# A gated cross-attention and ternary feed-forward kernel: normalised x split into bf16 halves before it is transposed, and transposed by DMA instead of on TensorE

## The reference

```python
def _L0_xattn_ref(hidden_states, encoder_hidden_states, Wq, Wk, Wv, Wo, gq, gk):
    q = (hidden_states @ Wq).reshape(B, Sq, H, D)          # 32 sequences of 100 rows, 512 wide; 16 heads of 128
    k = (encoder_hidden_states @ Wk).reshape(B, Skv, H, D) # 361 context rows, 256 wide
    v = (encoder_hidden_states @ Wv).reshape(B, Skv, H, D)
    q = rmsnorm(q, gq)
    k = rmsnorm(k, gk)
    scores = jnp.einsum('bqhd,bkhd->bhqk', q, k) * scale
    attn = jax.nn.softmax(scores, axis=-1)
    out = jnp.einsum('bhqk,bkhd->bqhd', attn, v)
    return out.reshape(B, Sq, H * D) @ Wo
x = x + jnp.tanh(g_xattn[0]) * _L0_xattn_ref(_layernorm(x, axis=-1), ctx_1024, ...)
x = x + jnp.tanh(g_ffn[0]) * _L0_ffn_ref(_layernorm(x, axis=-1), ...)
```

## Time and profile before

| | |
|---|---|
| time, median of 3 runs | 2481.73 us (2481.36 to 2483.34) |
| the profiled execution's own time | 2482.65 us |
| its span, first to last instruction | 2480.5 us |
| PE busy | 2256.4 us, 91% |
| DVE busy | 1903.3 us, 77% |
| ACT busy | 1577.8 us, 64% |
| POOL busy | 1200.9 us, 48% |
| float32 transposes of x on TensorE | 128, 18.0 us busy |
| mean granted TensorE clock | 0.970 of full |

### The profile page before, as it was taken

One profiled execution on the slowest core, in us unless ns is written; L12 is line 12 of the kernel. 1 busy time (PEld: TensorE's weight loads), 2 busy tenths in 40 slices (PEclk: granted clock), 3 DMA queues, 4 the chain that ended last, 5 costly groups with the idle time before them and its releaser, 6 DMA issues. The chain is left out here.

```text
span 2480.5 us, 52473 instructions
## 1 busy us (share of the span) xinstructions
PE 2256.4 (91%) x16482; PEld 1597.2 (64%) x16634; DVE 1903.3 (77%) x4175; ACT 1577.8 (64%) x3226; POOL 1200.9 (48%) x1538
## 2 busy tenths in 40 slices
PE   2599999999999999999999999999999995589998
PEld 1377777777677767677767777777777773344443
DVE  4588878877878787877787788778887773589996
ACT  3567666766666666666666676667676763744443
POOL 4365646565656565656565656565656551000000
PEclk8799999999999999999999999999999998799999
DMA  6466666666666656666666666666666653434443
GB/s 199 103 112 113 122 111 119 113 121 112 116 116 121 107 118 116 122 112 116 114 122 113 116 112 123 113 115 113 124 113 118 115 113 106 160 77 106 118 114 93
DMA packets 887466, 289.31 MB, mean 117 GB/s; under 512 B 847760, under 2 KB 859312, under 8 KB 886704
## 3 DMA queue, kind: packets, MB, share of 16 engines
q1 hardware_dynamic: 887216, 286.15, 60.0%
HBM read 63.21 MB, written 13.11 MB: 31 GB/s over the span
## 5 line engine op out<-in xcount | busy, mean ns | idle before, releaser
L747 DVE TENSOR_TENSOR khat<-keys_ps,krs 128x512 f32<-128x512 f32 (+1 forms) x384 | 263.4, 686 | 289.9 <-POOL krs L989 289.9
L995 POOL TENSOR_TENSOR ksplit<-khat,ksplit 128x512 bf16<-128x512 f32 (+1 forms) x384 | 444.0, 1158 | 59.8 <-ACT ksplit L549 59.1
L986 POOL TENSOR_SCALAR kvar<-kss 128x4 f32<-128x4 f32 (+1 forms) x384 | 86.2, 225 | 674.0 <-DVE kss L737 674.0
L989 POOL TENSOR_TENSOR krs<-kvar,minus_half 128x4 f32<-128x4 f32 (+1 forms) x384 | 387.0, 1008 | 32.0
L569 ACT ACTIVATE early<-score_ps,nbias,qrs 100x361 f32<-100x361 f32 x512 | 330.5, 651 | 91.0 <-DVE nbias L765 88.5
L578 ACT ACTIVATE psplit<-early,rden 100x361 bf16<-100x361 f32 x512 | 304.9, 596 | 83.0 <-DVE rden L771 81.5
L554 ACT ACTIVATE ksq<-keys_ps 128x512 f32<-128x512 f32 (+1 forms) x384 | 228.6, 596 | 202.4 <-PE keys_ps L25 201.1
L777 DVE SCALAR_TENSOR_TENSOR psplit<-early,rden,psplit 100x361 bf16<-100x361 f32 x512 | 323.1, 641 | 7.8 <-ACT psplit L578 3.7
L549 ACT ACTIVATE ksplit<-khat 128x512 bf16<-128x512 f32 (+1 forms) x384 | 240.2, 625 | 115.5 <-DVE khat L747 105.0
L23 PE MATMUL keys_ps<-wk_hi,ctxT 128*128 128x512 bf16 (+1 forms) x649 | 249.8, 385 | 62.0 <-DVE khat L747 40.6
L755 DVE TENSOR_REDUCE nmax<-score_ps 100x1 f32<-100x361 f32 x512 | 269.1, 526 | 45.9 <-PE score_ps L25 45.9
(11 more groups left out here) (155 smaller groups left out, 5295.6 us busy)
## 6 DMA issues: line engine op xcount, KB each, us to landing
ctx_raw<-in_ctx SPq DMA_DIRECT2D x31, 256.0 KB, 3.0
xin<-in_x SPq DMA_DIRECT2D x32, 200.0 KB
xres<-in_x SPq DMA_DIRECT2D x32, 200.0 KB
x_rows<-xres SPq DMA_DIRECT2D x32, 200.0 KB
xin<-x_rows SPq DMA_DIRECT2D x25, 256.0 KB, 2.8
xres<-x_rows SPq DMA_DIRECT2D x25, 256.0 KB, 2.6
out<-xres SPq DMA_DIRECT2D x25, 256.0 KB, 2.9
kT<-ksplit SPq DMA_TRANSPOSE x384, 3.1
```

Source lines behind the costliest of these rows:

```text
L747: dve.tensor_tensor(khat[0:KV[t], k, :].rearrange("p (h d) -> p h d", h=G), keys_ps[k][0:KV[t], :].rearrange("p (h d) -> p h d", h=G), rs, ...
L989: pool.tensor_tensor(krs[0:KV[t], k, :], kvar[0:KV[t], k, :], minus_half[0:KV[t], 0:G], ALU.pow).then_inc(krs_done, 1)
L995: pool.tensor_tensor(ksplit[0:KV[t], t, 1, :], khat[0:KV[t], (u + t) % 2, :], ksplit[0:KV[t], t, 0, :], ALU.subtract).then_inc(k_lo_done, 1)
```

## The change

ACT no longer reads x back from PSUM. It writes the high half of the normalised x into a new tile `xsplit` (`x_hi`), POOL subtracts it from x to make the low half (`x_lo`), and SP issues one DMA transpose for each of the two sequences (`turn_x`), which writes both halves into `xT`. The two ("x", b) entries leave the list of the shared banks. `queries` wait on the DMA's semaphore `xT_in` where they waited for the shared bank. `yT` takes the place in memory of `qsq`. POOL also clears `xsplit` at the start.

```diff
@@ shared_uses @@
-            order += [("x", 0), ("x", 1)]
...
-            if u == UNITS - 5 and not last:
-                order += [("x", 0)]
...
-            if u == UNITS - 5 and not last:
-                order += [("x", 1)]
@@ tiles @@
-        xT_hi, xT_lo = sb("xT_hi", [P, CM, QT], BF16), sb("xT_lo", [P, CM, QT], BF16)
+        xsplit = sb("xsplit", [SQR, 2, 2, DM], BF16)
+        xT = sb("xT", [P, 2, CM, 2, SQR], BF16)
-        yT = sb("yT", [P, NT, QT], F32)
+        assert NT == G
+        yT = qsq
@@ sync @@
+            def turn_x(j, b):
+
+                sp.wait_ge(x_lo_done, j * 2 + b + 1)
+                sp.sem_inc(sp_passed, 1)
+                sp.dma_start_transpose(xT[:, :, :, b, :].rearrange("p a c q -> p (a c) q"),
+                                       xsplit[:, b, :, :].rearrange("q a n -> q (a n)")).then_inc(xT_in[b], 16)
@@ sync, the loads of the weights, before the seventh @@
                     turn_ctx(0, 0, 0), turn_ctx(0, 1, 0)
+                    sp.wait_ge(x_zero, 1)
+                    turn_x(0, 0), turn_x(0, 1)
@@ sync, turn(i, u) @@
                 if has_keys(u, last):
                     turn_keys(i, u + 2, 0), turn_keys(i, u + 2, 1), turn_keys(i, u + 2, 2)
+                if not last and u == UNITS - 4:
+                    sp.wait_ge(shared_done, use(i, ("q", UNITS - 5, QD - 1))[0] + 1)
+                    sp.sem_inc(sp_passed, 1)
+                    turn_x(i + 1, 0), turn_x(i + 1, 1)
                 if has_scores(u, last):
                     turn_probs(i, u + 1, 0), turn_probs(i, u + 1, 1)
@@ tensor, queries @@
-                if hg == NG and k == 0:
-                    eng.wait_ge(shared_free, use(i, ("x", 1))[0] + 1)
+                if k == 0 and hg % NG == 0:
+                    for b in range(2):
+                        eng.wait_ge(xT_in[b], (i + 2) * 16)
@@ tensor, two_turns @@
-                if new_x:
-                    turn_x(i, 0)
                 if qu:
                     query_squares(i, u)
                 heads_out(i, v, 0), heads_out(i, v, 1)
-                if new_x:
-                    turn_x(i, 1)
@@ scalar @@
-            def turn_x_hi(i, b):
-                n, k = use(i, ("x", b))
-                eng.wait_ge(shared_done, n + 1)
-                copy(xT_hi[:, :, b * SQ:(b + 1) * SQ],
-                     shared_ps[k][:, 0:CM * SQ].rearrange("p (c q) -> p c q", c=CM)).then_inc(xT_hi_done, 1)
+            def x_hi(i, b):
+                n = (i + 1) * 2 + b + 1
+                eng.wait_ge(xhat_ready, n)
+                if not (isinstance(i, int) and i < 0):
+                    eng.wait_ge(xT_in[b], (i + 1) * 16)
+                copy(xsplit[0:SQ, b, 0, :], xin[:, b, :]).then_inc(x_hi_done, 1)
@@ vector, two_turns @@
                 if new_x:
-                    layernorm(i, 1), turn_x_lo(i, 0)
+                    layernorm(i, 1)
...
-                if new_x:
-                    turn_x_lo(i, 1)
@@ gpsimd @@
+            def x_lo(i, b):
+                n = (i + 1) * 2 + b + 1
+                eng.wait_ge(x_hi_done, n)
+                eng.sem_inc(pool_passed, 1)
+                pool.tensor_tensor(xsplit[0:SQ, b, 1, :], xin[:, b, :], xsplit[0:SQ, b, 0, :],
+                                   ALU.subtract).then_inc(x_lo_done, 1)
@@ gpsimd, two_turns @@
                 if kv:
                     keys_lo(i, v + 2, 1), keys_lo(i, v + 2, 2)
+                if u == UNITS - 5 and not last:
+                    x_lo(i, 0), x_lo(i, 1)
                 if new_ctx:
                     split_ctx(i + 1, b, 2, 1 - par, ctx_raw)
@@ gpsimd, start @@
+            pool.memset(xsplit[:, :, :, :], 0.0).then_inc(x_zero, 1)
```

More of the change, by code:

```diff
@@ L196, in attention_block @@
         x1_out = [sem(f"x1_out{b}") for b in range(2)]
-        nat_hi_done, nat_ready, nat_zero = sem("nat_hi_done"), sem("nat_ready"), sem("nat_zero")
+        nat_hi_done, nat_ready, nat_zero, x_zero = (sem(n) for n in ("nat_hi_done", "nat_ready", "nat_zero", "x_zero"))
         ctxT_in = [sem(f"ctxT_in{b}") for b in range(2)]
@@ L209, in attention_block @@
         shared_done, shared_free = sem("shared_done"), sem("shared_free")
-        xT_hi_done, u_hi_done = sem("xT_hi_done"), sem("u_hi_done")
+        x_hi_done, x_lo_done, u_hi_done = sem("x_hi_done"), sem("x_lo_done"), sem("u_hi_done")
+        xT_in = [sem(f"xT_in{b}") for b in range(2)]
         q_hi_done, q_sq_done, o_hi_done = sem("q_hi_done"), sem("q_sq_done"), sem("o_hi_done")
@@ L313, in turn @@
                     for b in range(2):
-                        sp.wait_ge(xT_hi_done, i * 2 + b + 1)
+                        sp.wait_ge(x_lo_done, i * 2 + b + 1)
                         load_x(i + 1, b, xin, x_in)
@@ L395, in mixed @@
                 last.then_inc(shared_done, 1)
[L397 to L402, removed]
             def queries(i, u, k):
@@ L413, in queries @@
                         last = product(pe, ps[:, j * QT:(j + 1) * QT], wq_hi[:, c, h * D:(h + 1) * D],
-                                       wq_lo[:, c, h * D:(h + 1) * D], xT_hi[:, c, :], xT_lo[:, c, :],
+                                       wq_lo[:, c, h * D:(h + 1) * D], xT[:, 0, c, :, 0:SQ], xT[:, 1, c, :, 0:SQ],
                                        c == 0, c == CM - 1)
@@ L477, in two_turns @@
                 kv, sv, mv = has_keys(v, last), has_scores(v, last), has_mixed(v, last)
-                new_x = u == UNITS - 5 and not last
                 if ku:
@@ L521, in _ @@
             eng.wait_ge(consts_ready, 5)
-            turn_x(-1, 0), turn_x(-1, 1)
             eng.wait_ge(w_lo_done, WK_PIECES)
@@ L656, in two_turns @@
                 if new_x:
-                    turn_x_hi(i, 0)
+                    x_hi(i, 0)
                 if su:
@@ L667, in two_turns @@
                 if new_x:
-                    turn_x_hi(i, 1)
+                    x_hi(i, 1)
                 if kv:
@@ L691, in _ @@
             act.activation(gate[:, :], g_row[:, 2:3], ACT.Tanh).then_inc(gate_ready, 1)
-            turn_x_hi(-1, 0), turn_x_hi(-1, 1)
+            x_hi(-1, 0), x_hi(-1, 1)
             def weights_hi(first, end):
@@ L786, in mixed_lo @@
                     uT_hi[:, c, :, cols]).then_inc(shared_free, 1)
[L788 to L793, removed]
             def x_stats(i, b):
@@ L939, in _ @@
             dve.tensor_tensor(gqk[:, :], g_row[:, 0:1], g_row[:, 1:2], ALU.mult).then_inc(gqk_ready, 1)
-            turn_x_lo(-1, 0), turn_x_lo(-1, 1)
             def weights_lo(first, end):
@@ L1069, in _ @@
             pool.memset(nat[:, :, :, KVT - 1, :, :], 0.0).then_inc(nat_zero, 1)
+            pool.memset(xsplit[:, :, :, :], 0.0).then_inc(x_zero, 1)
+            eng.wait_ge(x_zero, 1)
             eng.wait_ge(nat_zero, 1)
@@ L1082, in _ @@
             deviation(-1, 0), deviation(-1, 1)
+            x_lo(-1, 0), x_lo(-1, 1)
             for u in range(UNITS, UNITS + 2):
```

## The result

| | before | after |
|---|---|---|
| time, median of 7 runs each | 2481.73 us (2478.83 to 2486.68) | 2491.0 us (2489.0 to 2496.91) |
| ratio, with its 95% interval | | 1.004 (1.0027 to 1.0053) |
| span of the profiled execution | 2480.5 us | 2488.3 us |
| mean granted TensorE clock | 0.970 | 0.970 |

The prediction said 2472 with a range of 2448 to 2487. The time is outside the range and on the other side of no change.

What follows compares the result with a forecast made beforehand. TensorE was taken to bound the attention block. From the profiled 2482.65 us, -33.3 (turn 3's stretch), -7.4 (clock), +30 (wait for x) and +1.0 (start) gave 2472.95; 2472 for the median, range 2448 to 2487.

Steps and rivals of the forecast that it cites:

- TensorE's stretch and the clock in turn 3: Turn 3, x transposes to keys of block 2: 2.22 us a pair less, 33.3 saved; clock falls gone, 7.4 saved.
- The new wait: Queries of turn 5 wait 2.0 us a pair for x's DMA; 30 us lost, bounds 24 to 48.
- The weighting of 5 to 2: Turn 5's wait for x: 1.6 us in five pairs and 3.2 in two, weighted to 2.05, taken as 2.0.
- decision point of 2.65: Wait for x in us a pair, at the queries of turn 5, from which the change would be slower.
- The falls of the clock go: TensorE clock falls in turn 3 disappear with the x transposes; 7.4 us saved, bounds 0 and 7.4.
- The rival that named this: Clock falls stay, at the squares or at the new wait on TensorE: 2479 us, chance 0.15.
- The first rival: x lands too late for turn 5's queries every time, a wait of 3.2 in all pairs: 2490 us, chance 0.15.
- What stands behind x on SP: Probabilities' and context's transposes queued on SP behind x cost nothing; without the wait on x, the context is 0.1 late.
- Contention: POOL's work slows DVE's probs_lo by 0.63 us, hidden behind the wait on x; rival that it reaches POOL: 2481, 0.10.
- The page's price for the landing: x's DMA transpose would land after 2.5 us, making the sum 13 us better; rejected for the rows' 2.9 at best.
- The start: POOL's clearing of xsplit delays the first x by 0 to 1.8 us; 1.0 lost was taken.

Runs made afterwards that it cites:

- POOL's part early: Changed kernel with POOL's low halves of x made earlier, and queries reading the keys' weights without waiting for x; 2457.8 us, ratio 0.9906.
- both chains early: Changed kernel with POOL's low halves of x made earlier and SP's x transposes issued behind the keys' first; 2449.51 us, ratio 0.9867.
- the normalising moved as well: Kernel with both chains early, and DVE normalising the second sequence's x behind qvar, not ahead of it; 2436.0 us, ratio 0.9821.

## Why the prediction was wrong, step by step

*TensorE's stretch and the clock in turn 3*: right. -33.3 and -7.4 make -40.7; the turns 3 gave -40.8, with turn 3 at 30.99 where 31.0 was forecast.

*The new wait*: the mechanism, its place (`queries` of turn 5) and its cause (SP's own queue, with POOL over by then) were right; the size was not. The term was 15 x 2.0 = 30 and measured 38.9. Two numbers in it failed. The keys' third transpose goes out 428.15 - 418.91 = 9.24 after the keys of block 2 and not at 8.6. I took 8.6 from turn 5, where the last `keys_lo` ends at 8.46, as "the order without x transposes". But what was taken from TensorE in turn 3 was not taken from the chain over DVE and POOL. In turn 3 before, that transpose stood at 676.38 - 668.10 = 8.28 behind a TensorE that came 2.22 later, so had the chain not moved at all it would now stand at 10.5. It moved by somewhat more than half of that 2.22. The kernel before without the new x confirms it: there too the third transpose goes out at 9.25 in 14 of 15 pairs, with no x on POOL or SP.

What holds the chain back in turn 3 is seen beside the row biases on DVE (`nbias`, 100x1), between the keys of block 2 and `khat`:

```profile
421.50 0.76 DVE L765 TENSOR_TENSOR nbias<-nmax,qrs 100x1 f32<-100x1 f32 x1
422.74 0.61 DVE L765 TENSOR_TENSOR nbias<-nmax,qrs 100x1 f32<-100x1 f32 x1
...
421.09 1.15 POOL L985 TENSOR_TENSOR ksplit<-khat,ksplit 128x512 bf16<-128x512 f32 x1
422.67 0.67 POOL L1024 TENSOR_TENSOR nat<-ctx_raw,nat 128x256 bf16<-128x256 f32 x1
```

Each ends with POOL's subtraction beside it. In turn 5 of the kernel before they took 0.49 and 0.16, the second with POOL idle, and `khat` came 4.34 after the keys of block 2 where it now comes 423.94 - 418.91 = 5.03. No run moved these alone, so this cause is read from the rows and not tested. The rest is the landing: 3.2 in the median, where the sum had 2.9 for most pairs, and in three pairs longer waits, the longest 3.8. The weighting of 5 to 2 was not sound either: over all 15 pairs of the kernel before, the third transpose took 4.5 only in those two, which would have made the term 27. With the spacing of 1.51 and 1.40 that is 9.24 + 1.51 + 1.40 + 3.2 = 15.35, against the 12.89 at which the queries are wanted: 2.46, and the row says 2.41. So the mean of 2.6 sits just under the decision point of 2.65 that the prediction named for being slower. Each pair also lost 31.77 - 29.20 - 2.41 = 0.16 beside the wait, 2.4 in all.

*The falls of the clock go*: this is the step that failed in kind. In turn 3 they did go. But the prediction judged the new wait by the loop's end, where a gap had left the clock at 1.00. After the change the granted clock is 0.50, the lower of 1.2 and 2.4 GHz, behind four of the fifteen waits for x, and at four loop ends too (0.53 in the window at 616.77 above, where it was 1.00). Behind the wait that costs 33.34 - 31.77 = 1.57 and more each, together 49.2 - 38.9 - 2.4 = 7.9. The rival that named this (2479, at 0.15) held in mechanism together with the larger wait: it said that the new wait is another gap on TensorE, and it was.

Put together, for the profiled execution: 2472.95 + 8.9 + 2.4 + 7.9 = 2492.15, less 1.7 for the smaller rows of the table (-0.3 where +1.0 was forecast, +1.9, -2.3), is 2490.45; its own time is 2490.04. The first rival, x too late in all pairs, gave 2490 at 0.15, by waits of 3.2 with no falls. The time is its time, and that is luck: its reason was that each transpose may land like the one of 4.5, and the median landing is 3.2. The waits are longer than forecast for an earlier reason, the later start of the chain, and the clock makes up the rest.

*What stands behind x on SP*: nothing, as forecast, as long as the wait for x covers it. Uncovered, the context costs 0.8 and not 0.1 a pair.

*Contention*: charged to DVE, and rightly hidden behind the wait for x. The size was 0.63 by the earlier trace rows and is 1.9 (2.98 against 1.09). That POOL pays nothing, as the prediction took from the earlier trace rows, is wrong: its second subtraction starts while the first `probs_lo` still runs and takes 1.45 and not 1.16 in all 15 pairs, and with POOL's part early it takes 1.16. Here it changed nothing, since SP comes to x only after it.

*The page's price for the landing*, 2.5 us ("DMA: Bandwidth & Descriptors", Anatomy of one DMA, in the Trainium skill): that section's figures are for DMAs issued on GpSimd's path, and these go out from SP, so the prediction set them against the wrong kind of DMA. The 32 transposes of x took 2.9 to 4.6, and the rows were the right price.

*The start*: 1.0 lost was forecast, 0.3 was gained. *Behind the attention block*, where nothing was changed, 2.3 were gained. The profiled executions of the eight kernels have 433.9 to 436.0 there, against 439.2 and 436.9, so the change has no part in it that these runs can tell.

What stays open is why the clock falls behind some waits and not behind others of the same length, and at which loop ends. The runs show only where. The kernel before had six falls, all in turn 3. With both chains early there are two there and three at loop ends; with the normalising moved as well, and the wait for `qvar` gone, none is left in turn 3 and three at loop ends. Each count is of one execution.

## What to carry to other kernels

When work leaves the bounding engine, its successor has to arrive earlier by as much, and the feeding chain over the other engines doesn't move with it: take the chain's time from the turn that is changed and not from its sister without the extra work. When a value passes several queues in order, ask in each what stands ahead of it, and move it in all or in none. And count a new wait on TensorE dearer than its length, since the clock may fall behind it: here behind 4 of 15 waits, at about 1.6 us and more each.

## What was not expected of the hardware

Two of DVE's 100x361 instructions with two SBUF inputs take 1.09 us with POOL idle, 1.72 beside its work on the context and 2.98 beside two of its float32 subtractions. The trace shows more than a slowdown. In the attention block of the changed kernel 250 row biases start during one of POOL's subtractions of keys, context or x with at least 0.15 us of it to come. All but one of them end 0.01 to 0.02 us after that subtraction, up to 1.09 us after their start, where a row bias alone takes 0.16. So here a small DVE instruction with two SBUF inputs stands until POOL's subtraction is over, and it is dear on DVE's path to the keys even though its work is almost nothing. POOL pays too, when it comes second: 1.45 against 1.16.

And DMA transposes on SP's queue go out 1.40 to 1.51 us apart: 1.50 from the keys' second to their third, 1.40 from the first of x to the second. So a transpose stands about one and a half microseconds back for each one ahead, and in two of the 15 pairs, where those ahead landed late, the two of x stood 2.1 and 2.2 apart.
